# Layer 1 as one block, one step less per quantisation, and x of sequences 6 and 7 quantised like the others

## What is computed

```python
def fp4_quant_dequant(x):
    xb = x.reshape(shape[:-1] + (shape[-1] // BLOCK, BLOCK))
    scale = jnp.max(jnp.abs(xb), axis=-1, keepdims=True) / 6.0
    scale = jnp.maximum(scale, jnp.float32(1e-12))
    xn = xb / scale
    idx = jnp.searchsorted(_MID, jnp.abs(xn))
    return (_GRID[idx] * jnp.sign(xn) * scale).reshape(shape)

# layer 1
h = _layernorm(x) * (1 + ca) + sa
x = x + ga * attention(h, Wqkv, Wo)
h = _layernorm(x) * (1 + cb) + sb
gate, y = fp4_linear(h, w_gate), fp4_linear(h, w_up)
x = x + gb * fp4_linear(silu(gate) * y, w_down)
```

## Time and profile before

| | |
|---|---|
| time, median of 3 runs | 1257.5 us (1253.91 to 1260.66) |
| time of the profiled execution | 1258.3 us |
| its span, first to last instruction | 1256.4 us |
| mean granted TensorE clock | 0.870 |
| busy: PE, DVE, ACT, POOL | 963.4, 809.2, 638.5, 436.0 us |
| feed-forward of layer 1 | the last 143 us of the span |

### The profile page before, as it was taken

The page is one execution under the profiler, slowest core; times in us unless marked ns, Lnnn a source line. Parts: engine busy times, 40 slices in busy tenths (PEclk is TensorE's granted clock), DMA queues, the critical chain, the costliest instruction groups (busy, mean ns, idle before and its releaser), DMA issues. The chain is left out here.

```text
span 1256.4 us, 25141 instructions
## 1 busy us (share of the span) xinstructions
PE 963.4 (77%) x8604; PEld 655.8 (52%) x8604; DVE 809.2 (64%) x1683; ACT 638.5 (51%) x2132; POOL 436.0 (35%) x332
## 2 busy tenths in 40 slices
PE   6779899999999898998522489658618888856675
PEld 3456566565656565666521456345404555534564
DVE  5767967777685868673755835112224699769995
ACT  3465776767676767775100243212116888843322
POOL 2334433423333423330100378788730232300221
PEclk8789999999999999997555589878858999988867
DMA  7574343434344443431410223335530000000000
GB/s 202 150 187 105 89 120 99 117 96 108 90 115 105 112 103 92 124 98 34 124 23 1 76 69 75 63 60 113 77 80 1 2 1 1 2 1 9 17 17 25
DMA packets 89010, 93.62 MB, mean 75 GB/s; under 512 B 18801, under 2 KB 62305, under 8 KB 88945
## 3 DMA queue, kind: packets, MB, share of 16 engines
q1 hardware_dynamic: 78576, 84.12, 25.6%
q0 software_dynamic: 10368, 8.66, 4.8%
HBM read 24.36 MB, written 10.70 MB: 28 GB/s over the span
## 5 line engine op out<-in xcount | busy, mean ns | idle before, releaser
L835 POOL TENSOR_TENSOR qk_cos<-qk_raw,const 128x512 f32<-128x512 f32 x128 | 183.7, 1436 | 312.5 <-ACT qk_raw L589 312.5
L575 ACT ACTIVATE prob<-psS,neg_max 128x96 f32<-128x96 f32 x512 | 167.9, 342 | 84.3 <-DVE neg_max L670 83.5
L442 PE MATMUL psQ<-a_xnT,weights 128*128 128x512 f32 x250 | 148.6, 679 | 2.4 <-ACT a_xnT L621 1.6
L550 PEld LDWEIGHTS psO<-probT,v_windows 96*64 96x64 f32 x2048 | 74.0, 144 | 140.3 <-ACT probT L649 120.4
L685 DVE TENSOR_TENSOR qk_roped<-qk_cos,qk_swapped 128x512 f32<-128x512 f32 x128 | 119.6, 935 | 5.9 <-DVE qk_swapped L676 5.5
L550 PE MATMUL psO<-probT,v_windows 96*64 96x64 f32 x2048 | 92.2, 235 | 40.3 <-ACT probT L649 40.0
L1497 POOL DMA_INDIRECT ex_rows<-rows,ex_index x64 | 67.4, 1053 | 122.0 <-DMA ex_index<-lists 103.1
L1508 POOL DMA_INDIRECT sums<-ex_y,ex_index x64 | 98.7, 1542 | 23.9 <-issue 18.6
L575 ACT ACTIVATION_READ_ACCUMULATOR prob<-psS,neg_max 128x1 f32 x512 | 105.5, 206 | 0.0
L649 ACT COPY probT<-psT 96x512 f32<-96x512 f32 x128 | 76.8, 600 | 46.5 <-PE psT L530 46.5
L589 ACT COPY qk_raw<-psQ 128x512 f32<-128x512 f32 x125 | 73.9, 591 | 46.9 <-PE psQ L442 46.8
(11 more groups left out here) (317 smaller groups left out, 1929.2 us busy)
## 6 DMA issues: line engine op xcount, KB each, us to landing
qk_swapped<-qk_raw SPq DMA_DIRECT2D x512, 64.0 KB, 2.0
v_windows<-v_tok SPq DMA_DIRECT2D x32, 384.0 KB, 4.5
v_windows<-v_tok SPq DMA_DIRECT2D x32, 256.0 KB, 3.6
mod<-mod_rows SPq DMA_DIRECT2D x12, 512.0 KB, 7.0
ex_w<-in_L_ffn_W SPq DMA_DIRECT2D x16, 256.0 KB, 3.2
v_windows<-v_tok SPq DMA_DIRECT2D x32, 96.0 KB, 2.1
rows<-rt_h SPq DMA_DIRECT2D x8, 256.0 KB, 2.4
sums<-rt_zeros SPq DMA_DIRECT2D x8, 256.0 KB, 2.7
```

What stands on the lines that cost most here:

```text
L442: last = nc.tensor.matmul(bank, k.wqkvT[:, col:col + P], xnT[:, :], start=True, stop=True)
L550: ins = nc.tensor.matmul(psO[D * j:D * j + D, i * P + a * HALF:i * P + (a + 1) * HALF], vw[:, par, a, t, hd], probT[:, 2 * j + i, a * HALF ...
L575: last = nc.scalar.activation(prob[:, s, 2 * j + i, :], psS[:, s, j, i * KW:(i + 1) * KW], ACT.Exp, bias=nmax[:, s, 2 * j + i:2 * j + i + ...
L835: nc.gpsimd.tensor_tensor(rcos[:, half, :], raw[:, half, :], k.const[:, K_COS:K_COS + T], ALU.mult).then_inc(cos_done, 1)
```

## The change

A quantisation has nine steps. The `and` keeps two exponent bits and is followed, in the same instruction, by an `or` with a constant: read as a float, the result is 1.5 x 2^23 or 2^24 for values from 2 and from 4 on, and tiny below. The two rounding steps take the maximum with 1.5 x 2^22 in place of a product. Since the second subtracts the sum from the constant, the sign turns, and the scale is made negative to turn it back. `fp4` with its list of jobs is gone; all quantisations are generators of `fp4_steps`.

`phase_attention1` and `phase_ffn1` are one block, `phase_layer1`. The feed-forward takes PSUM banks that attention has done with: gate and up those of the scores, the turned hidden activations those of the turned probabilities and of the attention output, x that of the projections. The hidden scratch lies in the modulation of layer 0. TensorE turns x of sequence 0 in turn 7, and multiplies gate and up for sequence 0 before and after the last output projection; ScalarE copies them around the last head scaling. Statistics and normalisation of sequence 6 come in turn 7, those of sequence 7 behind its residual, and both sequences are normalised on ScalarE. x of sequence 6 is quantised on VectorE before the residual of sequence 7, x of sequence 7 step by step beside the hidden activations in feed-forward turn 1.

```diff
-EXPONENT = 0x7F800000
 MAGIC = 1.5 * 2.0 ** 22
+BINADE, RAISE = 0x40800000, 0x0B400000
 BELOW = 1.0 - 2.0 ** -23
...
+def fp4_steps(nc, dve, own, q, signal, ready=None, taken=None, out_free=None):
...
+    if ready:
+        dve.wait_ge(*ready)
     done = own.mark(v.tensor_reduce(q.amax, q.source_blocks, AX.X, ALU.max, apply_absolute_value=True))
-    done = own.mark(v.tensor_scalar(q.scale, q.amax, 1.0 / 6.0, 1e-12, ALU.mult, ALU.max))
+    done = own.mark(v.tensor_scalar(q.scale, q.amax, -1.0 / 6.0, -1e-12, ALU.mult, ALU.min))
     done = own.mark(v.reciprocal(q.inv, q.scale))
-    done = own.mark(v.tensor_scalar(q.inv, q.inv, BELOW, None, ALU.mult))
+    done = own.mark(v.tensor_scalar(q.inv, q.inv, -BELOW, None, ALU.mult))
-    v.tensor_tensor(q.xn_blocks, q.source_blocks, q.inv_wide, ALU.mult).then_inc(taken, 1)
+    scaled = v.tensor_tensor(q.xn_blocks, q.source_blocks, q.inv_wide, ALU.mult)
+    if taken:
+        scaled.then_inc(taken[0], 1)
+    else:
+        taken = own.sem, own.mark(scaled)
-    dve.wait_ge(taken, b + 1)
-    done = own.mark(v.tensor_scalar(q.binade.bitcast(U32), q.xn.bitcast(U32), EXPONENT, None, ALU.bitwise_and))
+    dve.wait_ge(*taken)
+    done = own.mark(v.tensor_scalar(q.binade.bitcast(U32), q.xn.bitcast(U32), BINADE, RAISE, ALU.bitwise_and, ALU.bitwise_or))
-    done = own.mark(v.tensor_scalar(q.binade, q.binade, 1.0, None, ALU.max))
+    done = own.mark(v.scalar_tensor_tensor(out=q.total, in0=q.binade, scalar=MAGIC, in1=q.xn, op0=ALU.max, op1=ALU.add))
-    done = own.mark(v.scalar_tensor_tensor(out=q.total, in0=q.binade, scalar=MAGIC, in1=q.xn, op0=ALU.mult, op1=ALU.add))
+    done = own.mark(v.scalar_tensor_tensor(out=q.total, in0=q.binade, scalar=MAGIC, in1=q.total, op0=ALU.max, op1=ALU.subtract))
-    done = own.mark(v.scalar_tensor_tensor(out=q.total, in0=q.binade, scalar=-MAGIC, in1=q.total, op0=ALU.mult, op1=ALU.add))
-    own.mark(v.tensor_tensor(q.out_blocks, q.total_blocks, q.scale_wide, ALU.mult))
-
-
-FP4_SIGNALS = 9
+    if out_free:
+        wait(dve, *out_free)
+    v.tensor_tensor(q.out_blocks, q.total_blocks, q.scale_wide, ALU.mult).then_inc(signal, 1)
...
+        xqT, silu, up = sb("f1_xqT", [C, T]), sb("f1_silu", [P, 2, TILES, F1]), sb("f1_up", [P, 2, TILES, F1])
+        hq, hqT, fmul = sb("f1_hq", [P, TILES, F1]), sb("f1_hqT", [P, 3, T]), sb("f1_ymul", [P, TILES, C])
+        spent = k.mod0[:, 0:GB, :, :].rearrange("p m b c -> p (m b c)")
+        h_bufs = [spent[:, i * TILES * F1:(i + 1) * TILES * F1] for i in range(3)]
+        h_bufs += [sb(f"f1h_{t}", [P, TILES * F1 // BLK]) for t in ("amax", "scale", "inv")]
+        psG, psU, psHT = [psS[i][0] for i in range(2)], [psS[i][1] for i in range(2)], [psT, psO]
...
+            def turn_xq(b):
+                pe.wait_ge(quantised2, b + 1)
+                if b < 2:
+                    pe.wait_ge(y_scaled, B - 1 + b)
+                wait(pe, xqT_ready, b)
+                for t in range(TILES):
+                    last = nc.tensor.transpose(psQ[:, t * P:(t + 1) * P], k.total[:, b, t, :], k.ident)
+                last.then_inc(f_turned, 1)
+            def gate_up(b, tiles):
+                pe.wait_ge(xqT_ready, b + 1)
+                for t in tiles:
+                    n = b * TILES + t
+                    if n < 2:
+                        pe.wait_ge(exp_done, (B * TILES - 1 + n) * H1)
+                    wait(pe, gate_out, n - 1)
+                    nc.tensor.matmul(psG[t % 2][:, 0:F1], xqT[:, t * P:(t + 1) * P], k.wgT[:, :], start=True, stop=True)
+                    nc.tensor.matmul(psU[t % 2][:, 0:F1], xqT[:, t * P:(t + 1) * P], k.wuT[:, :],
+                                     start=True, stop=True).then_inc(gated, 1)
...
+                    if t == 2 and not next1:
+                        turn_xq(0)
...
+            gate_up(0, range(2))
+            out_project(B - 1, (B - 1) % 2)
+            gate_up(0, range(2, TILES))
+            turn_xq(1)
+            for b in range(B):
+                if b + 1 < B:
+                    gate_up(b + 1, range(TILES))
+                if b + 2 < B:
+                    turn_xq(b + 2)
+                down(b)
...
-                    if t == 3 and 0 <= b - 1 < EARLY:
+                    if t == 3 and not first:
                         normalise2(b - 1)
...
+            gates(0, range(2))
+            scale_y(B - 1)
+            gates(0, range(2, TILES))
+            copy_xqT(1)
+            for b in range(B):
+                if b + 1 < B:
+                    gates(b + 1, range(TILES))
+                if b == 0:
+                    normalise2(B - 1)
+                if b + 2 < B:
+                    copy_xqT(b + 2)
+                copy_hqT(b)
...
+            norm2.root_bias(pool, B - 1)
+            modulate2(B - 1)
+            for b in range(B):
+                pool.wait_ge(f_read, b + 1)
+                nc.gpsimd.tensor_tensor(k.x[:, b, :, :], k.x[:, b, :, :], fmul[:, :, :], ALU.add).then_inc(f_sum, 1)
...
-                    if u == 5 and 0 <= b - 1 < EARLY:
+                    if u == 5 and not first:
                         finish2(b - 1)
-                    for _ in range((0, 0, 2, 2, 0, 1, 3, 2)[u]):
+                    for _ in range((0, 0, 2, 2, 0, 1, 2, 2)[u]):
...
-                if not next1:
-                    reciprocals(b)
-                    for _ in residual(b):
-                        pass
...
-def phase_ffn1(nc, k):
...
+            reciprocals(B - 1)
+            for _ in quantise2(B - 2):
+                pass
+            for _ in residual(B - 1):
+                pass
+            finish2(B - 1)
             for b in range(B):
+                product(b)
+                later = quantise2(B - 1) if b == 1 else iter(())
+                for _ in quantise_hidden(b):
+                    next(later, None)
+                next(later, None)
+                if b > 0:
+                    gate_down(b - 1)
+            gate_down(B - 1)
```

More of the change, by code:

```diff
@@ L1277, in quantise @@
         dve.wait_ge(self.ld, 16 * 7)
-        last, = fp4(self.nc, dve, self.own, [Fp4(self.w[:, :], self.q[:, :], self.WIDTH, self.bufs)])
-        last.then_inc(self.quantised, 1)
+        for _ in fp4_steps(self.nc, dve, self.own, Fp4(self.w[:, :], self.q[:, :], self.WIDTH, self.bufs), self.quantised):
+            pass
     def take(self, dve):
@@ L1714, in out_project @@
                 wait(pe, y_read, b)
+                if b == B - 1:
+                    pe.wait_ge(xqT_ready, 1)
                 for t in range(TILES):
@@ L1853, in body @@
                     norm.root_bias(pool, b + 2)
-                if 0 <= b - 1 < EARLY:
+                if not first:
                     norm2.root_bias(pool, b - 1)
@@ L1930, in body @@
             def body(b, par, first, next1, next2):
-                steps = quantise2(b - 2) if 0 <= b - 2 < EARLY else iter(())
+                steps = quantise2(b - 2) if b >= 2 else iter(())
                 added = iter(()) if first else residual(b - 1)
@@ L2159, in phase_store @@
-def phase_store(nc, k):
-    with ExitStack() as ctx:
-        block = ctx.enter_context(nc.Block())
-        @block.sync
-        def _(sp):
-            for b in range(B):
-                sp.dma_start(k.out[b].rearrange("(t p) c -> p t c", p=P), k.x[:, b, :, :]).then_inc(k.stored, 16)
-            sp.wait_ge(k.stored, 16 * B)
-STOP = 9
+            reciprocals(B - 1)
+            for _ in quantise2(B - 2):
+                pass
+            for _ in residual(B - 1):
+                pass
+            finish2(B - 1)
```

294 lines of the change are left out of this document (68 added, 226 removed).

## The result

The changed kernel takes **1236.58 us** (median of four runs, 1235.22 to 1238.12) against 1258.1 for four runs of the kernel before: a ratio of 0.9829, 95% interval 0.9805 to 0.9852, or 18.6 to 24.5 us less. 1238.6 was forecast, with 1232 to 1247 around it. The profiled execution took 1236.25 us, span 1234.5.

What follows compares the result with a forecast made beforehand. Layer 1 was taken to be bound by VectorE. The terms -7.4, -1.8, -9.2, -2.1 and +0.8 sum to -19.7, from 1258.3 to 1238.6 us, with a range of 1232 to 1247.

Steps and rivals of the forecast that it cites:

- One step less: Hidden quantisation on VectorE in the feed-forward: the removed step saves 0.92 us eight times, -7.4 us.
- that rival: Two bit operations in one VectorE instruction halve its rate: 7.4 us more, 1246 us; chance 0.07.
- The attention: Attention turns of layer 1: the removed step has a pitch of 0.46 us and counts in four turns, -1.8 us.
- x of sequences 6 and 7: Feed-forward: two turns lose 11.8 us of extra work, sequence 7 brings 2.6 back in turn 1; together -9.2 us.
- GpSimd beside turn 0: Feed-forward turn 0: GpSimd's two multiply-adds for sequence 7 could hold VectorE 0 to 1.9 us; taken as 0.
- The attention row: Earlier trace, attention turn: a VectorE step took 1.39 us beside GpSimd's 1.60, against 0.69 alone.
- The meeting: Attention's end to first feed-forward product: 7.98 us idle goes, a wait of about 4 comes; product at 1120.2, -2.1 us.
- TensorE's path: Feed-forward: slow projections make VectorE wait 0.8 us in three of six turns, an old 1.56 us wait goes; +0.8 us.
- The tail: Last hidden quantisation to the end of the span: the forecast sum had no term for it.

Runs made afterwards that it cites:

- e_best: Changed kernel with GpSimd modulating sequence 7 beside turn 1, its x quantised in turn 2, and sequence 6 modulated by VectorE: 1237.50 us, ratio 0.9845.

## Why the prediction was right, and where not

- **One step less, -7.4 in the feed-forward:** a plain turn went from 13.50 to 12.57, eight times 0.93. Right, and shown by putting the step back. The second bit operation cost nothing (0.88 us), so that rival is out.
- **The attention, -1.8:** from r0 to the reciprocals of sequence 6 117.32 became 116.20, -1.1, and with ten steps it was 117.32 again. Right in kind, sized too large: a turn now takes 19.79 us, as long as turn 1, which never had a quantisation (19.80). That suggests another limit close behind; no run shows which.
- **x of sequences 6 and 7, -9.2:** turns 3 to 5 of before were 11.8 longer than plain ones, turn 1 is now 2.78 longer: -9.0. Right; no run took this part alone.
- **GpSimd beside turn 0, taken as 0:** this is the step that failed. Turn 0 took 13.85 instead of 11.98, **+1.9**, the upper end of the bounds. I had read from the earlier trace rows that in the feed-forward GpSimd pays and VectorE does not. That row was a product that had begun first; e_best shows the same product paying when GpSimd began first. The attention row (1.39 for 0.69) was the right one.
- **The meeting, -2.1:** from r7 to the first product -3.5, of which 0.4 is the later r7. Mechanism right (the wait for GpSimd, 2.96 us; no wait for gates), the chain from statistics to maximum 6.3 us rather than 7.3: without attention work beside it GpSimd took 0.29 us for the bias and 1.27 for the multiplication, not 0.67 and 1.77, and ScalarE began 0.3 us sooner. What the overlap hides is 8.5 us.
- **TensorE's path, +0.8:** a slow projection (5.37 us) did make a product wait (1.13 for the 0.8 forecast), but in one turn of one trace and in none of the other, not in three of six. Nor do slow and fast projections alternate in the trace of before: turns 4 and 5 were both slow. With the old wait gone, -0.4 in the first trace. The frequency was wrong; e_best shows how near the mechanism is.
- **The tail, 0:** -2.2 in the first trace, +0.2 in the second.

The sum of the first trace: -0.6 up to r0, -4.2 to the first product, -15.0 in the feed-forward (-7.4, -9.0, +1.9, -0.4), -2.2 at the end, 21.9 by span. Forecast were 19.7. The steps that were off, in the order of the list: +0.7 in the attention, +0.2, +1.9 for GpSimd, -1.0 at the meeting, -1.2 on TensorE's path, -2.2 at the tail, and -0.6 up to r0. They partly cancel: the 1.9 us for GpSimd are set off by terms that had nothing to do with them, 2.8 of these at the tail and up to r0, where another execution comes out otherwise. That the total fits this well is in part luck.

## What to carry to other kernels

When one engine sets a stage, count its instructions turn by turn: the plain turn came out at 12.57 us for a forecast of 12.6, turn 1 at 15.35 for 15.2. What such a count misses is the neighbours, here GpSimd's 1.9 us in turn 0. By the medians the same step was worth 11.6 us in the merged block (1248.21 against 1236.58) and 3 to 6 in the old ones; in the traces 1.5 to 2.1 us of the difference are a product that waited where a shorter turn met another engine's slow path. Work that moves to GpSimd "for free" must be placed by what VectorE runs beside it, and by who starts first. Before believing a gain of 1 or 2 us, look at a second trace of the same kernel: the stage you edited should move, the others should not.
